# Attention stage of a two-layer kernel: the three PSUM copies of each first-layer expert tile move from VectorE to ScalarE

## The reference, cut to what matters

```
xn = layernorm(x)
x = x + attention(xn) + experts(xn)

# attention: q, k, v = xn @ w_qkv.T ; softmax(q k^T / 4, causal) v ; @ w_o.T
# experts (each token's two best):
h   = silu(x_tile @ W1[e])          # 256 -> 128
out = combine * (h @ W2[e])         # 128 -> 256
```

## Time and profile before

| what | us |
|---|---|
| median of three runs | 1144.94 |
| the three runs | 1138.82, 1144.94, 1145.24 |
| span of the profiled execution | 1041.1 |
| median less span | 103.8 |
| expert tiles inside the attention stage | about 192 to 581 in the span |

### The profile page before, as it was taken

One profiled execution on the slowest core, in us unless ns is written; L12 is line 12 of the kernel. 1 busy time (PEld: TensorE's weight loads), 2 busy tenths in 40 slices (PEclk: granted clock), 3 DMA queues, 4 the chain that ended last, 5 costly groups with the idle time before them and its releaser, 6 DMA issues. The chain is left out here.

```text
span 1041.1 us, 18530 instructions
## 1 busy us (share of the span) xinstructions
PE 905.0 (87%) x6218; PEld 489.7 (47%) x6219; DVE 671.0 (64%) x1560; ACT 423.5 (41%) x736; POOL 323.6 (31%) x415
## 2 busy tenths in 40 slices
PE   1876799999999999999999999879982799997764
PEld 1622233444444445445444322667440687786542
DVE  7485799887777786787877762768142444443444
ACT  1542155555655555565555668221120233331000
POOL 6045720022222223222221155002776000002775
PEclk9998699999999999999999999989997899999796
DMA  9457613030127401182111122900222344443443
GB/s 336 175 167 199 197 45 113 19 116 31 58 75 160 128 31 57 33 161 95 32 32 33 31 68 76 353 7 23 104 101 96 115 154 157 151 155 101 124 132 114
DMA packets 83748, 113.44 MB, mean 109 GB/s; under 512 B 12304, under 2 KB 71696, under 8 KB 83152
## 3 DMA queue, kind: packets, MB, share of 16 engines
q1 hardware_dynamic: 64720, 68.26, 22.2%
q0 software_dynamic: 13728, 37.50, 11.4%
q10 hardware_dynamic: 5216, 6.58, 1.9%
HBM read 58.11 MB, written 54.00 MB: 108 GB/s over the span
## 5 line engine op out<-in xcount | busy, mean ns | idle before, releaser
L757 ACT ACTIVATE probs<-ps_st 128x1024 f32<-128x1024 f32 (+3 forms) x320 | 286.4, 897 | 245.8 <-PE ps_st L909 126.6
L810 DVE TENSOR_REDUCE part_max<-ps_row 128x1 f32<-128x512 f32 (+3 forms) x560 | 350.3, 669 | 54.9 <-PE ps_row L925 28.2
L925 PE MATMUL ps_row<-ks,qs 96*128 96x512 bf16 (+3 forms) x640 | 188.9, 358 | 17.6 <-PEq L259 7.6
L906 PE MATMUL ps_st<-qs,ks 99*128 99x512 bf16 (+3 forms) x640 | 181.8, 354 | 4.2 <-DMA qs<-max_parts 3.9
L870 PE MATMUL ps_o<-probs,v_all 128*17 128x256 f32 (+1 forms) x2432 | 176.4, 362 | 0.0
L1126 POOL DMA_INDIRECT moe_yg<-yd,slot x64 | 61.9, 967 | 168.6 <-DMA yd<-moe_ys 149.4
L906 PEld LDWEIGHTS ps_st<-qs,ks 99*128 99x128 bf16 x640 | 47.0, 97 | 128.1 <-ACT probs L757 59.9
L925 PEld LDWEIGHTS ps_row<-ks,qs 96*128 96x128 bf16 x640 | 63.3, 99 | 75.9 <-DVE part_max L810 33.4
L1276 POOL DMA_INDIRECT xd<-xn,slot x64 | 64.3, 1005 | 89.2 <-DVE slot L198 70.0
L870 PEld LDWEIGHTS ps_o<-probs,v_all 128*17 128x17 f32 x2432 | 40.4, 95 | 92.8 <-issue 88.1
L1157 PE MATMUL moe_ps_h<-w,moe_xs_t 128*128 x316 | 82.7, 384 | 0.1
(11 more groups left out here) (214 smaller groups left out, 1227.6 us busy)
## 6 DMA issues: line engine op xcount, KB each, us to landing
xd<-zeros SPq DMA_DIRECT2D x6, 2048.0 KB, 14.0
moe_xs<-xd SPq DMA_DIRECT2D x79, 128.0 KB, 2.1
yd<-moe_ys SPq DMA_DIRECT2D x79, 128.0 KB, 1.9
qk_parts<-o_t SPq DMA_DIRECT2D x16, 384.0 KB, 3.0
moe_xs<-xd POOLq DMA_DIRECT2D x47, 128.0 KB, 2.4
yd<-moe_ys POOLq DMA_DIRECT2D x47, 128.0 KB, 2.0
qs<-qk_parts SPq DMA_DIRECT2D x84, 64.0 KB, 2.4
ks<-qk_parts SPq DMA_DIRECT2D x18, 256.0 KB, 9.2
```

Source lines behind the costliest of these rows:

```text
L757: act.activation(probs[:, at % NPB, :, off:CH], ps_st[at % 2][:, :, off:CH], ACT.Exp, scale=HD ** -0.5).then_inc(exp_done, 1)
L810: dve.tensor_reduce(part_max[reduced % 2][:, h:h + k, i, j:j + 1], bank[:, 0:k * w].rearrange("p (h w) -> p h w", h=k), AX_X, ALU.max).the ...
L906: mm = pe.matmul(ps_st[n % 2][:, h, off:CH], ks[g % 2][:, q, k * P:(k + 1) * P], qs[c][:, q, off:CH], start=True, stop=not diagonal)
L925: mm = pe.matmul(cols, qs[c][0:KROWS, h, i * P:(i + 1) * P], ks[g % 2][0:KROWS, h, j * CH:j * CH + w], start=True, stop=(j < c))
```

## The change

The three copies of every expert tile are removed from VectorE's program and put into ScalarE's, at the same places of the plan: directly behind the exponential that precedes them, and behind `copy_output` where that is emitted there. A new semaphore `moe_copied` counts them. The waits of TensorE and of GpSimd's queue for these three kinds of row now name it; those for max and turn rows still name `row_used`, which counts only these now. Line numbers behind the change are a few higher (L757 is L762, L744 is L749, L768 and L769 are L773 and L774, L810 is L819, L925 is L936, L948 is L959, L954 is L965, L960 is L971, L965 is L976; the new copies are L778, L783 and L789).

```
--- before.py
+++ after.py
@@ -645,6 +645,7 @@
         x_in = [l.sem(f"moe0_x_in{b}") for b in range(XB)]
         y_out = [l.sem(f"moe0_y_out{b}") for b in range(XB)]
         h_used, hid_ready = l.sem("moe0_h_used"), l.sem("moe0_hid_ready")
+        moe_copied = l.sem("moe0_copied")
         gathered = [l.sem(f"moe0_gathered{b}") for b in range(2)]
         summed = l.sem("moe0_summed")
         block = ctx.enter_context(nc.Block())
@@ -655,7 +656,11 @@
 
         def used(n):
 
-            return sum(u[0] != "h" for u in rows[:n + 1])
+            return sum(u[0] in ("max", "turn") for u in rows[:n + 1])
+
+        def copied(n):
+
+            return sum(u[0] in ("x", "g", "y") for u in rows[:n + 1])
 
         @block.sync
         def _(sp):
@@ -723,7 +728,7 @@
                                        ALU.mult).then_inc(hid_ready, 1)
                 j = slot - 3
                 if j >= 0:
-                    pool.wait_ge(row_used, used(row_of["y", j]))
+                    pool.wait_ge(moe_copied, copied(row_of["y", j]))
                     pool.dma_start(m.yd0[j * P:(j + 1) * P, :], ys[:, j % XB, :]).then_inc(y_out[j % XB], 16)
             for b in range(XB):
                 pool.wait_ge(y_out[b], 16 * len(range(b, NT0, XB)))
@@ -767,6 +772,21 @@
                     bank = ps_row[row_of["h", j] % NSM]
                     act.activation(h_tanh[:, j % 2, :], bank[:, 0:HID], ACT.Tanh, scale=0.5)
                     act.copy(h_copy[:, j % 2, :], bank[:, 0:HID]).then_inc(h_used, 1)
+                elif u[0] == "x":
+                    j = u[1]
+                    act.wait_ge(row_done, row_of["x", j] + 1)
+                    act.copy(xs_t[:, j % 2, :, :], ps_row[row_of["x", j] % NSM][:, 0:D].rearrange(
+                        "p (k t) -> p k t", k=KH)).then_inc(moe_copied, 1)
+                elif u[0] == "g":
+                    j = u[1]
+                    act.wait_ge(row_done, row_of["g", j] + 1)
+                    act.copy(hid_t[:, j % 2, :], ps_row[row_of["g", j] % NSM][:, 0:P]).then_inc(moe_copied, 1)
+                elif u[0] == "y":
+                    j = u[1]
+                    act.wait_ge(row_done, row_of["y", j] + 1)
+                    if j >= XB:
+                        act.wait_ge(y_out[j % XB], 16 * (j // XB))
+                    act.copy(ys[:, j % XB, :], ps_row[row_of["y", j] % NSM][:, 0:D]).then_inc(moe_copied, 1)
             copy_output(len(exps) - 1)
 
         @block.vector
@@ -785,22 +805,11 @@
                         dve.wait_ge(summed, i * TOP0 + k + 1)
                     continue
                 n += 1
-                if u[0] == "h":
+                if u[0] in ("x", "h", "g", "y"):
                     continue
                 dve.wait_ge(row_done, n + 1)
                 bank = ps_row[n % NSM]
-                if u[0] == "x":
-                    dve.tensor_copy(xs_t[:, u[1] % 2, :, :],
-                                    bank[:, 0:D].rearrange("p (k t) -> p k t", k=KH)).then_inc(row_used, 1)
-                elif u[0] == "g":
-                    dve.tensor_copy(hid_t[:, u[1] % 2, :], bank[:, 0:P]).then_inc(row_used, 1)
-                elif u[0] == "y":
-                    j = u[1]
-                    if j >= XB:
-
-                        dve.wait_ge(y_out[j % XB], 16 * (j // XB))
-                    dve.tensor_copy(ys[:, j % XB, :], bank[:, 0:D]).then_inc(row_used, 1)
-                elif u[0] == "max":
+                if u[0] == "max":
                     g, c, pieces = u[1:]
                     h, i, j, w = pieces[0]
                     k = len(pieces)
@@ -883,6 +892,8 @@
                 before = rows[n - NSM]
                 if before[0] == "h":
                     pe.wait_ge(h_used, before[1] + 1)
+                elif before[0] in ("x", "g", "y"):
+                    pe.wait_ge(moe_copied, copied(n - NSM))
                 else:
                     pe.wait_ge(row_used, used(n - NSM))
 
@@ -949,7 +960,7 @@
                 elif u[0] == "h":
                     j = u[1]
                     bank_free(n)
-                    pe.wait_ge(row_used, used(row_of["x", j]))
+                    pe.wait_ge(moe_copied, copied(row_of["x", j]))
                     for k in range(KH):
                         mm = pe.matmul(bank[:, 0:HID], xs_t[:, j % 2, k, :], m.w1[:, k, bass.ds(experts[j], 1), :],
                                        start=(k == 0), stop=(k == KH - 1))
@@ -961,7 +972,7 @@
                 else:
                     j = u[1]
                     bank_free(n)
-                    pe.wait_ge(row_used, used(row_of["g", j]))
+                    pe.wait_ge(moe_copied, copied(row_of["g", j]))
                     mm = pe.matmul(bank[:, 0:D], hid_t[:, j % 2, :], m.w2[:, bass.ds(experts.pop(j), 1), :],
                                    start=True, stop=True)
                 mm.then_inc(row_done, 1)
```

5 lines of the change are left out of this document (3 added, 2 removed).

## The result

| comparison and kernel | us | ratio to the kernel before, same comparison |
|---|---|---|
| first: kernel before, 4 runs | 1141.88 (1137.11 to 1145.24) | |
| first: changed kernel, 4 runs | 1154.58 (1149.03 to 1159.42) | 1.0127 [1.0078, 1.0176] |
| second: changed kernel, 6 runs (before: 1044.73) | 1051.33 | 1.0058 [1.0040, 1.0076] |
| fourth: changed kernel, 12 runs (before: 1139.67) | 1148.72 | 1.0080 [1.0052, 1.0109] |

The change makes the kernel slower: in all three comparisons the interval lies above 1, and the medians are 0.6 to 1.3% apart. I forecast 1151.0 us and +6.1. The range of 1142 to 1159 held the first comparison's time of 1154.58, but its difference, +12.7, is twice the forecast and lies outside the forecast's own +3 to +11. The two later comparisons, with more runs, gave +6.6 and +9.1. (The second, third and fourth comparison ran on three different chips.)

A forecast was written before the change was run, and what follows sets the result against it. TensorE, 99% busy in the expert tiles' stretch, was taken to bound the kernel there. New waits of 9.3 us less 3.2 us gained made +6.1, so 1144.94 became 1151.0 us; range 1142 to 1159.

The forecast's parts named there:

- TensorE bounds the stretch: Expert tiles: TensorE's matmuls busy 99% at full clock, so other engines' edits count only through TensorE's waits.
- The copies' prices: Moved copies on ScalarE: 0.373 us for 256 columns, 0.270 for 128; 47.8 us added there, 53.5 leave VectorE.
- Eight behind an output copy: Eight moved copies queued on ScalarE behind an output copy: banks free 0.62 to 0.74 us late each, 5.3 us.
- Four with three rows behind: Four moved copies whose bank is wanted three rows later, before the next exponential unit: late, 2.6 us together.
- Thirteen others: Late copies behind short diagonal units or straight behind a first-kind site: 3.1 us, 1.4 after 1.7 comes off.
- New waits: TensorE waiting for small banks at 25 late ones of 141 moved copies: 5.3 + 2.6 + 1.4 = 9.3 us.
- Hand-over of 0.2 us at h rows: Time assumed from a ScalarE copy's end to the h or y row's matmul; 0.1 for other rows.
- Gain of 3.2 us: TensorE waits less for VectorE's reductions once copies leave VectorE; three in five such waits cured, at most 5.8 us.
- The next exponential waits for nothing: ScalarE's exponential behind a moved copy starts some 0.2 us later, but TensorE asks for it only two units on.
- +6.1 in all: Whole kernel: new waits of 9.3 us less a gain of 3.2 us, slower by 6.1 us.
- second rival: Usual sites tip over: copies end 0.2 us later than reckoned, 67 sites late, +13.9 us, 1158.8 us; chance 0.14.
- The sum on 1144.94: Forecast +6.1 us added to the shown median 1144.94, taken as span 1041.1 plus 103.8 us around it: 1151.0 us.

The follow-up runs named there:

- the 25 copies back on VectorE: Changed kernel with the 25 copies the prediction called late made by VectorE again, the other 116 on ScalarE: ratio 1.0010, stretch 386.35 us.
- the doubled kernel: Changed kernel with a second, unused copy on ScalarE ahead of every moved copy: ratio 1.0167, stretch 404.40 us.
- alone: Kernel before with the three copies on VectorE cut to one column each and nothing added on ScalarE: ratio 0.9998, stretch 385.02 us.
- everything ahead: Changed kernel with ScalarE's x, g, y copies and h rows' tanh and copy made ahead of the preceding exponential: 0.9972, again 0.9960; stretch 382.97, 382.96 us.

## Why the prediction was right

- **TensorE bounds the stretch.** Right. Its clock stayed full, and 8.5 of its 10.1 us of upward steps stand at the banks that its subtraction picked out.
- **The copies' prices.** I took 0.373 and 0.270 us; they are 0.369 and 0.263. The loads that I made of them were off: ScalarE rose by 32.6 us, not 47.8, and VectorE fell by 41.9, not 53.5. The busy time counts once what two instructions share, and at tile 9 the moved copy starts 0.10 us ahead of the end of the one before it (290.48 to 290.58). No step of the sum used these loads.
- **Eight behind an output copy, 5.3 us.** All eight are there; 4.9 us. The place was shown by the output copy behind them (three sites left with 0.07 to 0.09 us, five with nothing).
- **Four with three rows behind, 2.6 us.** All four; 2.4 us: 0.77 each at g of tiles 1 and 31, 0.43 each at y of tiles 12 and 19.
- **Thirteen others, 1.4 us.** Six of them show, 1.2 us together, of which x of tile 2 has 0.62 and x of tile 11 has 0.23. Seven show nothing.
- **New waits, 9.3 us.** 8.5 us at the sites. Another 1.5 us are the 17 small steps at max rows, for which the sum had no term. 1.1 us of them are the longer h and y rows just ahead of them; with the 25 copies back on VectorE all 17 are gone.
- **Hand-over of 0.2 us at h rows.** It is 0.14: from 290.86 to 291.00 at tile 9, from 337.86 to 338.00 in the doubled kernel. Usual x-to-h sites showed no step, as forecast, and had twice the margin that I reckoned (0.26 less 0.2).
- **Gain of 3.2 us, three in five of the reductions' waits.** The step that was mis-sized. It measured 1.9 alone and about 2.2 in the changed kernel. The waits on VectorE's reductions shrank from 10.1 to 6.5 us at L936 and L945, where I had said some 5, and a wait of the load is not a wait of the matmul: the PE rows of L936 on the reductions stand at 1.2 us before and 1.4 after.
- **The next exponential waits for nothing.** Right. With everything ahead of it, it even starts 0.5 us later at tile 9 without harm.
- **+6.1 in all.** In the stretch it is 8.5 + 1.6 - 2.5 = +7.6, against 9.3 - 3.2: by a gain about 1 us too large and the small steps left out. The +12.7 of the first comparison comes close to the second rival's +13.9, but not by its mechanism: no usual x-to-h site shows a step. That the time of that comparison fell into the range owes something to the range's width.
- **The sum on 1144.94 with 103.8 us "around the span".** Wrong reading, without effect on the difference. In every execution whose time and span are both shown the time is the span plus 1.7 us (1159.42 and 1157.7). So the shown span of 1041.1 us most likely belongs to an execution of about 1043 us, without the pauses described below.

The queue order is what decides: at tile 9 a filled bank waited 1.3 us (289.16 to 290.48) behind two instructions that didn't need it. The Trainium skill, "PSUM — Partial Sum Buffer", Engine vs sequencer instructions, has ScalarE's queue as strict FIFO. The trace agrees by that row.

The Trainium skill, "Perfetto Trace Analysis", Optimizing Scalar/DVE Operations, says that offloading some work to ScalarE may make sense if VectorE is saturated. At 77% VectorE was not saturated, and the move is worth 1.6 us here with the copy placed well and costs 7.6 us placed badly. The overheads that the prediction took from the same section, 51 and 125 ns, lie 74 ns apart; the copies of 256 columns lie 51 to 55 ns apart (373 or 369 against 424).

Open is why the first comparison gave 1.0127. The interval's lower end, 1.0078, lies inside the 1.0052 to 1.0109 of the fourth comparison, the kernel and the stretch are the same, and there were four runs against twelve; the spread of four runs may be all of it. Against a further cost in the stretches of the pauses described below speaks the fourth comparison, whose kernel before was as slow (1139.67) and which gave 1.0080. No experiment rules out a cost elsewhere on the first chip.

## What to carry to other kernels

Before moving a copy between engines, ask not how busy the engine is but what stands in its queue at that moment, and when the buffer that the copy frees is next wanted; subtract the two for every site. If a short copy and a long instruction are ready about together, and the long one has slack, put the short one ahead: here the order alone was worth 11.5 us of 394.5 (about 2.3 of them by older copies), against 1.6 for the move itself. Count also what a late row costs beyond its wait: its weight load no longer runs ahead of it, and the row itself lasted up to 0.1 us longer. And read the waits on that engine's own existing copies first, since they tell what a new one in the same place will cost.

## What the runs showed that I had not expected

In three of the four comparisons the kernel before took about 1140 us, in the second 1045, and all kernels there were as much shorter. The changed kernel's windows in either case, up to the first x row, the stretch, up to the last exponential, and the rest; the first trace:

```profile
92.60:217.50 124.90, 90.97 (x638) 33.06 (x639) 88.69 (x155) 37.85 (x43) 33.23 (x36) 0.80 0.30 91
...
612.10:709.50 97.40, 72.89 (x619) 21.01 (x617) 39.82 (x74) 52.64 (x58) 31.33 (x33) 0.82 0.16 46
709.50:1157.70 448.20, 328.24 (x1409) 236.06 (x1405) 187.87 (x573) 81.77 (x222) 124.00 (x129) 0.86 0.34 110
```

and in the second comparison:

```profile
93.30:193.20 99.90, 88.21 (x639) 32.77 (x640) 87.82 (x155) 37.85 (x43) 33.30 (x36) 0.90 0.40 113
193.20:587.70 394.50, 384.01 (x3398) 176.49 (x3397) 256.87 (x444) 251.38 (x468) 95.84 (x183) 1.00 0.26 70
587.70:658.10 70.40, 68.08 (x619) 20.79 (x617) 39.93 (x74) 52.33 (x58) 31.25 (x33) 0.98 0.22 63
658.10:1051.40 393.30, 315.48 (x1409) 231.81 (x1405) 187.90 (x573) 82.05 (x222) 125.66 (x129) 0.91 0.39 125
```

VectorE, ScalarE and GpSimd do the same work in nearly the same busy time; the 107 us between them (25.0 + 27.0 + 54.9 by these rows) are idle, and lie in the three stretches that hold GpSimd's indirect transfers, with TensorE's granted clock lower in each (0.80 against 0.90 in the first). None lies in the stretch of the change. One such pause in the first trace's timeline:

```profile
116.94 0.61 PE L936 MATMUL ps_row<-ks,qs 96*128 96x512 bf16 x1 [5.02 <-DVE part_max L819]
...
123.92 0.69 DVE L819 TENSOR_REDUCE part_max<-ps_row 128x2 f32<-128x512 f32 x1 [7.03 <-remote]
124.67 0.10 PEld L936 LDWEIGHTS ps_row<-ks,qs 96*128 96x128 bf16 x1 [7.62 <-DVE part_max L819]
```

VectorE's reduction, its input ready, started 7 us late, and TensorE behind it stood still. The longest wait of this kind at L936 in the same stage of the trace of the second comparison is 1.4 us. What pauses the engine isn't shown, nor why the second comparison is free of it. It is a warning all the same: the profile ahead of the prediction had come from an execution some 100 us shorter than those that were timed, which an execution's time beside its span would have told.
